# The inputs of the state scans made on VectorE instead of GpSimd, in mixers 1 to 3 of a two-layer network

## The reference

```python
u = silu(conv3(xc)); dBC = u @ xproj_W
dlt, Bp, Cp = split(dBC); delta = softplus(dlt @ dt_W + dt_b)
def step(state, inp):              # state: (images, 384 channels, 16 states), over the 9 tokens
    u_l, d_l, B_l, C_l = inp
    k1 = A[None] * state + B_l[:, None, :] * u_l[:, :, None]
    state = state + d_l[:, :, None] * k1
    y_l = einsum('bdn,bn->bd', state, C_l)
    return state, y_l
y = (ys + u * D_param) * silu(z);  out_tok = y @ out_W     # then bilinear upsampling, added to x
```

## Time and profile before

| what | us |
|---|---|
| median of 3 runs | 1238.72 (1238.28, 1238.72, 1242.39) |
| the profiled execution | 1234.36 |
| its span in the trace | 1232.5 |
| TensorE's mean granted clock | 0.919 of full speed |
| VectorE busy | 736.2 of the span |
| GpSimd busy | 385.2 of the span |

### The profile page before, as it was taken

One profiled execution on the slowest core, in us unless ns is written; L12 is line 12 of the kernel. 1 busy time (PEld: TensorE's weight loads), 2 busy tenths in 40 slices (PEclk: granted clock), 3 DMA queues, 4 the chain that ended last, 5 costly groups with the idle time before them and its releaser, 6 DMA issues. The chain is left out here.

```text
span 1232.5 us, 18128 instructions
## 1 busy us (share of the span) xinstructions
PE 1058.5 (86%) x5916; PEld 889.5 (72%) x5916; DVE 736.2 (60%) x1414; ACT 475.3 (39%) x987; POOL 385.2 (31%) x304
## 2 busy tenths in 40 slices
PE   6876788789888997798788999889878999999975
PEld 4554688679887786788687667667757888888853
DVE  5676667977555567976584434665448434444327
ACT  3371136423223336224512434733552344443333
POOL 1105136434531125212202333631332443333411
PEclk9976798899888998898889999999988999999995
DMA  8327248676785386666544366552662589996557
GB/s 285 119 65 245 81 133 293 209 235 226 255 263 189 127 278 216 227 232 221 206 179 182 135 207 227 197 194 90 224 234 85 204 320 328 361 330 223 194 201 270
DMA packets 93365, 261.59 MB, mean 212 GB/s; under 512 B 10024, under 2 KB 46856, under 8 KB 77408
## 3 DMA queue, kind: packets, MB, share of 16 engines
q1 hardware_dynamic: 54760, 147.44, 34.4%
q10 hardware_dynamic: 23608, 63.19, 15.2%
q0 software_dynamic: 14912, 49.82, 11.4%
HBM read 168.59 MB, written 91.82 MB: 211 GB/s over the span
## 5 line engine op out<-in xcount | busy, mean ns | idle before, releaser
L602 POOL TENSOR_TENSOR sb_ring<-sb_raw,sb_ring 128x1024 fp32r<-128x1024 f32 x48 | 124.9, 2608 | 252.0 <-ACT sb_ring L1170 223.8
L662 PE MATMUL ps<-sb_xnH,sb_ring 128*128 128x288 f32 x512 | 170.1, 332 | 38.4 <-DMA sb_ring<-w_dram 18.3
L955 PE MATMUL ps<-sb_w,sb_xtH 128*128 x344 | 153.7, 447 | 14.7 <-DVE sb_hh L1803 12.6
L625 POOL DMA_INDIRECT y_dram<-sb_ysb,sb_target x86 | 87.2, 1014 | 243.1 <-ACT sb_ysb L1260 234.5
L663 PE MATMUL ps<-sb_xnH,sb_ring 128*128 128x288 f32 x512 | 160.6, 314 | 0.0
L664 PE MATMUL ps<-sb_xnL,sb_ring 128*128 128x288 f32 x512 | 160.5, 313 | 0.0
L1796 DVE TENSOR_TENSOR sb_xtL<-ps,sb_xtH 128x512 fp32r<-128x512 f32 x86 | 59.4, 691 | 139.6 <-ACT sb_xtH L1240 139.2
L957 PE MATMUL ps<-sb_w,sb_xtH 128*128 x344 | 139.1, 404 | 0.0
L956 PE MATMUL ps<-sb_w,sb_xtL 128*128 x344 | 138.7, 403 | 0.0
L662 PEld LDWEIGHTS ps<-sb_xnH,sb_ring 128*128 128x128 f32 x512 | 105.5, 206 | 45.1 <-DMA sb_ring<-w_dram 19.7
L616 POOL DMA_INDIRECT sb_xs<-xn_dram,sb_source x86 | 87.7, 1020 | 66.4 <-DVE sb_source L1707 34.7
(11 more groups left out here) (243 smaller groups left out, 2333.6 us busy)
## 6 DMA issues: line engine op xcount, KB each, us to landing
w_dram<-sb_ring SPq DMA_DIRECT2D x48, 1024.0 KB, 6.7
sb_w<-w_dram SPq DMA_DIRECT2D x48, 1024.0 KB, 7.2
sb_ring<-w_dram ACTq DMA_DIRECT2D x24, 1024.0 KB, 6.5
sb_raw<-in_w_ffn SPq DMA_DIRECT2D x24, 512.0 KB, 4.4
sb_raw<-in_w_ffn SPq DMA_DIRECT2D x48, 256.0 KB, 4.7
sb_X<-in_x SPq DMA_DIRECT2D x16, 576.0 KB, 8.8
xn_dram<-sb_XN ACTq DMA_DIRECT2D x18, 512.0 KB, 3.5
sb_g<-y_dram ACTq DMA_DIRECT2D x18, 512.0 KB, 9.5
```

The source lines that it names most:

```text
L602: pool.tensor_tensor(to[:, 1, :], raw[:, r % 2, :], to[:, 0, :].bitcast(f32), ALU.subtract)\
L625: pool.indirect_dma_start(y_dram[h], bass.IndirectOffsetOnAxis(ap=target[:, h, m:m + 1], axis=0), ysb[:, r, :], None).then_inc(y_stored[r] ...
L662: pe.matmul(out_ap, w[0], xh, start=start, stop=False)
L955: pe.matmul(PS[:, 1, :], xtH[:, i % 2, k, :], wh, start=k == 0, stop=False)
```

## The change

GpSimd's loop over j and part in the mixer goes, with its waits. VectorE calls `inputs` in every mixer. The list `order` of mixers 1 to 3 gets the three stages (inputs, 0), (inputs, 1) and (inputs, 2) and so has 12 instead of 9, over the same 18 slots. The ScalarE program, the buffers and the semaphores stay. `inputs` itself is unchanged: it waits for du_ready at the first, and for `scanned` of the same part of j - 1.

```diff
--- before.py
+++ after.py
@@ -557,17 +557,6 @@
                 yield step(1)
                 pool.wait_ge(veh_ready, c + 1)
                 pool.tensor_tensor(rsh[:, :], veh[:, :], half_neg[0:TT, 0:1], ALU.pow).then_inc(rsh_ready, 1)
-                for j in range(JC if c else 0):
-                    for part in range(2):
-                        yield step(15 + 6 * j - 2 * (j > 0) + part)
-                        if j == 0 and part == 0:
-                            pool.wait_ge(du_ready, c + 1)
-                            pool.wait_ge(bc_in, 16 * (c + 1))
-                        if j:
-                            pool.wait_ge(scanned, c * 2 * JC + 2 * (j - 1) + part + 1)
-                        ns = slice(part * NS // 2, (part + 1) * NS // 2)
-                        pool.tensor_tensor(db[:, ns, :], du[:, j:j + 1, :].broadcast_to((P, NS // 2, TT)), Bb[:, ns, :],
-                                           ALU.mult).then_inc(db_ready, 1)
                 if l == 0:
                     for g in range(FC):
                         yield step(63 - (1 - h) * 13 + 11 * g - 11 * g * h)
@@ -1483,7 +1472,8 @@
 
                 order = [(inputs, 0), (scan, 0), (inputs, 1), (weigh, 0), (scan, 1), (inputs, 2), (weigh, 1), (scan, 2),
                          (weigh, 2), (total, 2)] if c == 0 else [
-                    (scan, 0), (weigh, 0), (scan, 1), (total, 0), (weigh, 1), (scan, 2), (total, 1), (weigh, 2), (total, 2)]
+                    (inputs, 0), (scan, 0), (inputs, 1), (weigh, 0), (scan, 1), (total, 0), (inputs, 2), (weigh, 1),
+                    (scan, 2), (total, 1), (weigh, 2), (total, 2)]
                 for i, (stage, j) in enumerate(order):
                     for part in range(2):
                         yield step(17 + (2 * i + part) * 18 // (2 * len(order)))
```

## The result

| | before | after | ratio (95% interval) |
|---|---|---|---|
| median of 20 runs each, us | 1237.78 | 1242.41 | 1.0038 (1.0021 to 1.0054) |
| lowest and highest, us | 1229.42, 1243.77 | 1236.95, 1249.46 | |
| the profiled execution, us | 1234.36 | 1244.16 | |

The kernel became 4.6 us slower. The forecast was 1241.1 us, and the time lies in the range of 1233.5 to 1247.5. A difference between these two traces is therefore not yet an effect of the change.

The account below looks back on a forecast made before the run. It took VectorE to set the pace in mixers 1 and 2, and a TensorE, ScalarE and VectorE ring in mixer 3. -0.4 + 0 + 2.8 = +2.4 us on the three-run median gave 1241.1 us, range 1233.5 to 1247.5.

Parts of the forecast that it names:

- its two signs of being wrong: Mixer 1's stretch from first scan to yz changing by over 2.5 us, or inputs well over 1 us on average.
- The work added and the stretching that goes: VectorE, mixers 1 to 3: 13.5 us of inputs added, 13.5 us of stretching gone; -0.3, -1.6, +1.9 by mixer.
- What remains stretched: Mixer 1: L602 still stretches VectorE by 8 us, 0.4 per instruction; 2.4 us for six inputs, kept only in bounds.
- the walk: Scan stages of mixers 1 to 3 followed in program order by durations, with blocks where L602 stands; sum +2.4 us.
- the fourth rival: L602 on GpSimd holds up VectorE's new inputs: 4.2 us in mixer 1, half in mixer 2; 1247.4 us, chance 0.07.
- mixer 1's walk: Mixer 1: totals about 2 us earlier, mostly lost again, yz 0.4 us earlier; -0.4, bounds -2.5 and +2.4.
- spends 2 x 0.75, and its next step waits for TensorE: Mixer 1's first scan: its 2.47 us wait for GpSimd goes, but nothing is gained; 0, bounds -1 and +1.
- late gates: Rival, mixers 1 to 3: later totals delay ScalarE's gates and what follows; +7.7 us, 1246.4 us, chance 0.18.
- Mixer 2: Mixer 2: sg 0.5 us earlier, yz some 1.7 later, TensorE arriving about then; 0, bounds -1.5 and +1.7.
- Mixer 3: Mixer 3: early gain at tiles 17 to 19, then sb_hh up to 2.8 us late; +2.8, bounds 0 and +4.5.
- Silence wins: Rival: mixers 1 and 2 keep the gain from GpSimd's silence, mixer 3 at 0; -4 us, 1234.7 us, chance 0.20.
- covered: Rival: TensorE's slack in mixers 1 and 2 and mixer 3's ring hide both signs; 0, 1238.7 us, chance 0.17.

Follow-up runs that it names:

- m3: Kernel before with the change, 12-stage list included, in mixer 3 alone; 1.0011 (0.9988 to 1.0033) of before.
- zero_a: Changed kernel with L602's subtraction on GpSimd replaced by a memset that reads nothing; 0.9786 of before, median 1209.64 us.
- zero_b: Kernel before with L602's subtraction on GpSimd replaced by a memset that reads nothing; 0.9713 of before, median 1201.2 us.
- m1: Kernel before with the change, 12-stage list included, in mixer 1 alone; 0.9999 (0.9983 to 1.0016) of before.
- mix: Kernel before with VectorE making inputs in mixer 1 (old slots) and mixer 2 (list of 12), GpSimd in mixer 3; 0.9992 of before.
- both: Changed kernel with GpSimd also multiplying inputs, into a spare tile nobody reads; 1.0071 (1.0044 to 1.0099) of before.
- noinputs: Kernel before with the input products of mixers 1 to 3 left out, one memset per mixer instead; 0.9854 of before.

## Why the prediction was right, and where it was not

The time is in the range, and the forecast missed it by 1.3 us. Its sum of +2.4 us was about half of the 4.6 measured, though; it was laid on the median of three runs, 1238.72, where twenty gave 1237.78, and that 0.9 brought the forecast nearer. It had given 0.52 to a difference under 3.7 us and 0.32 to a larger loss, and by the medians the larger loss came. The signs it named came: no L569, GpSimd at 354.5 us, VectorE 3.8 us from 736.2, in mixer 3 scans at 1.35 and weightings at 0.75 us and a wait for the gates 2.2 us longer. Of its two signs of being wrong, mixer 1's stretch from first scan to yz changed by +1.4 us, not 2.5, and the inputs took 0.98 us on average, but 1.43 in mixer 1, which is the stretching by L602 that the sign stood for.

**The work added and the stretching that goes** came out as summed. VectorE's instructions in mixers 1, 2 and 3, from sb_dx to sb_yz (mixer 3 here from its own sb_dx too), add up to 52.2, 54.4 and 34.8 us before and 52.3, 52.5 and 37.0 after: 0, -1.9 and +2.2, where the sums said -0.3, -1.6 and +1.9. In mixer 1 the forms differ from the plan and the sum does not: scans +0.7, weightings -5.1, itL -4.0, inputs +8.6.

**What remains stretched** was the term that I took at nothing in the walk. It came to 4.1 us on the inputs of mixer 1 (8.6 - 4.5), the size that the fourth rival gave it (4.2), at 225.85. It still didn't become that rival's loss, since the weightings and itL are hardly stretched any more. What L602 stretches is 8.8 us in all after (scans 4.3, inputs 4.1, itL 0.3), where the prediction had 8: it moved, and it neither went nor grew. My figure for it was right as a total and wrong as a per-instruction share.

**The step that failed is mixer 1's walk**, -0.4 with bounds -2.5 and +2.4. Measured is 58.4 and 58.6 in the two kernels with the change there, against 56.7, 56.7 and 56.9 in the three without: +1.8, inside the bounds. The clock over it is 0.85 in before and in after, so it is not the clock's. By the windows view, which counts overlapping instructions once, VectorE is busy for 49.47 us in before and 49.13 in after, so the whole +1.8 is idle time. Three of its waits in before, beside the 2.47 of the earlier trace rows, are these:

```profile
205.27 0.45 DVE L1751 TENSOR_TENSOR sb_sg<-sb_sg,ps 128x288 f32<-128x288 f32 x1 [0.49 <-PE ps L664]
...
209.69 0.50 DVE L1756 TENSOR_TENSOR sb_itL<-sb_sg,sb_itH 128x288 fp32r<-128x288 f32 x1 [2.09 <-ACT sb_itH L1211]
...
227.37 0.46 DVE L1756 TENSOR_TENSOR sb_itL<-sb_sg,sb_itH 128x288 fp32r<-128x288 f32 x1 [1.68 <-ACT sb_itH L1211]
```

In after 2.47 for GpSimd before the first scan is 1.59 for the DMA of sb_Bb; the wait for TensorE at the next sg is 2.90, where it was 0.49; the first itL's is 1.75 where it was 2.09; the one at 223.97, of 2.71, was 1.68. Together 6.7 became 9.0. I had the second as "spends 2 x 0.75, and its next step waits for TensorE" and counted the two at 0 with +1 as the bound: they rose from 2.96 to 4.49, +1.5. The first scan's wait was not removed, it moved to the next step. In the middle I had won 2 us; the gates came 0.9 earlier, not 2. From the gates to sb_yz the stage then took 29.4 us instead of 26.6, where I had charged 1.6 in all (2 won, 0.4 left). The longer idle time for the itL behind the gates, 1.1 in the walk, came as 1.0. What the walk didn't have is that the two inputs of j = 2 stand in one piece beside two L591 for 5.52 us, 4.1 more than alone, and ScalarE's itH (231.77) waits 3.73 for the sg behind them. The rival "late gates" is not this: the gates were not late in mixer 1.

**Mixer 2**, forecast 0: 54.1, 57.2 and 54.5 with the change, 56.1, 54.2, 54.2 and 54.3 without. Means 55.3 and 54.7; not resolved.

**Mixer 3**, forecast +2.8. Tile by tile, counted from tile 17's first transpose, the starts of sb_hh of tiles 17 to 22 moved in after by -0.8, +0.1, +0.8, +1.3, +2.4 and +3.2 us against before, where the walk had -0.9, -1.2, +0.5, +1.2, +2.4 and +2.8. The stage took 52.0 and 52.1 in m3, after and zero_a, against 49.3 in before and 49.4 in zero_b: +2.7. That looks like a hit to a tenth, and is less than that. The windows over the stage in before, and in m1, where mixer 3 is unchanged, then in m3:

```profile
767.08:816.35 49.27, 40.25 (x187) 31.67 (x185) 34.09 (x51) 31.24 (x87) 26.84 (x22) 0.97 0.53 190
```

```profile
761.97:814.02 52.05, 43.00 (x188) 33.95 (x186) 34.17 (x50) 31.39 (x87) 26.79 (x22) 0.90 0.51 180
```

```profile
767.35:819.42 52.07, 42.37 (x187) 32.58 (x185) 35.75 (x57) 31.21 (x86) 17.51 (x16) 0.93 0.51 180
```

The same code took 49.27 us at a clock of 0.97 and 52.05 at 0.90, and TensorE's busy time makes 2.75 of the 2.78. At 0.93 an unchanged mixer 3 took 50.7 (mix) and a changed one 52.0. That gives the change +1.4, and so do the means (six unchanged traces 50.6, with zero_b, since no L602 runs beside mixer 3; three changed 52.0); m3's time says +1.4 too, with an interval of -1.5 to +4.1 us. The clock stood at 0.93 in all three changed traces, but the change doesn't fix it there: the run both, which has the change and GpSimd's products as well, ran at 0.97. The windows of mix and of the run both:

```profile
768.27:818.96 50.69, 41.83 (x188) 32.81 (x186) 33.91 (x50) 31.65 (x87) 26.78 (x22) 0.93 0.53 184
```

```profile
775.02:826.57 51.55, 40.70 (x187) 31.54 (x185) 37.09 (x57) 31.36 (x87) 24.71 (x22) 0.97 0.51 182
```

So at 0.97 the changed form took 2.3 us more than before, with VectorE 1.4 us busier than in after by GpSimd's products. One place shows why the clock hides a part of the change. From sb_hh of tile 20 to that of tile 21 before took 4.84 us at a clock of 1.00, mix 6.04 at 0.72, after 5.98 at 0.71 and the run both 5.95 at 1.00: the slower clock or the pair of scans that the walk had there each cost 1.1 to 1.2 us, and together no more. The change's own share in mixer 3 thus lies between 1.4 and about 2.3 us, and 2.8 was too large by 0.5 to 1.4. The mechanism (a pair of scans and two totals ahead of sb_hh, idle time that covers only the first inputs) is seen tile by tile: the -0.8 at tile 17 stands in all three changed traces and in no unchanged one (0.0 to +0.1), and against mix the six tiles are at -0.8, 0.0, +0.8, +1.2, +1.2 and +1.8. The walk's -1.2 at tile 18 did not come.

**The sum.** +1.8, the unresolved +0.6 and +1.4 to +2.3 make +3.8 to +4.7, beside the measured 4.6 (2.6 to 6.7); the forecast had -0.4, 0 and +2.8. So the forecast came as near as it did partly by luck: mixer 1's error and mixer 3's were of opposite sign. "Silence wins" was wrong as a total, though noinputs and both show that its mechanism has a price; "covered" is excluded by the interval; "late gates" is wrong on mixer 1's, and in mixer 3, where its condition held (the gates 2.3 us later), the cost was +1.4 to +2.3, not +4.

## What to carry to other kernels

When work moves off an engine that stretches another's instructions, ask which other instruction of it stays: the stretching moves to whatever now stands beside that one. Here only its total over the stage came out as predicted, and only while that other instruction stayed. Getting rid of a wait is worth only what the next step doesn't wait for instead, so walk one step further than the wait. Measure a stage of 50 us in several traces of unchanged code before a difference of 1 to 3 us in it is given to a change, and read the granted clock beside each.

## What the runs showed of the hardware

An unchanged stretch of this kernel took 49.3 to 52.1 us in six traces, and the granted clock over it was 0.97 to 0.90: a single trace is as uncertain as the whole change is large.

A GpSimd memset of 128x1024 f32 took 0.956 us (zero_b), and the weightings, scans and itL beside one in zero_a kept their lengths; the subtraction with two SBUF inputs on the same tile takes 2.6 us (before), and with it gone the whole kernel is 35 us (2.9%) shorter. With the inputs gone instead (noinputs) it is 18 us shorter, 6 of them in a later stage. So of GpSimd's work beside the mixers that subtraction costs this kernel more than the inputs do.
